# A graph block: rank and packed-edge tiles of 128 lanes in place of 125, and edge sends that use all of them

## The chip, the cores and the metric

The kernel runs on one core of a Trainium2 chip. The metric is the device time of one execution in microseconds (us); lower is better. The core has five engines that run side by side: TensorE (PE in the profile, its weight loads PEld), VectorE (DVE), ScalarE (ACT), GpSimd (POOL) and SyncE (SP), and 16 DMA engines that move data for all of them.

## The reference, cut to what matters

A block over a graph of 6,250 nodes with 256 features and 100,000 edges (`src`, `dst`), sorted by `dst`. Three of its steps read neighbours:

```
agg = segment_sum(relu(x[src]), dst)            # twice, in two graph convolutions, edges by dst
e   = exp(leaky_relu(el[src] + er[dst]))        # once, graph attention, grouped by src
out[src] += e / rowsum[src] * x[dst]
```

Between them stand dense steps on all nodes: two small MLPs, a mixing step, a linear layer with a layer norm, linear attention, and at the end a mixture of experts. The convolutions want the edges in the order of `dst`, the graph attention wants them in the order of `src`.

## The kernel before, in words

The 6,250 nodes are 49 tiles of 128 rows, the last one with 106 (`TAIL`). The kernel is a chain of stages (class `Stage`); at the end of each stage all engines meet at a barrier (line 48), so a stage lasts until its slowest engine is through.

An edge is one 32-bit word, `src << 13 | dst`. All 100,000 words lie in the tile `packed`, 125 partitions ("lanes", `LANES`) by 800 columns (`COLS`), written by VectorE at the end of `stage_load` (lines 281 to 283). The place that each edge takes in the list ordered by `src` is its rank. VectorE and TensorE work it out during the first convolution and leave it in `rank_i`, 125 by 800 too (line 1143).

The edges are then written out in that order, one column at a time: `send_columns` (line 676) issues on GpSimd an indirect DMA (a scatter) per column, with 125 indices from `rank_i[:, j]` and 125 words of 4 bytes from `packed[:, j]`, to `edges_by_src` in DRAM. The 800 columns are dealt out by hand to nine dense stages that otherwise leave GpSimd free; the calls in `stages_before_attention` (lines 2571 to 2583) give first column and count:

```python
stage_mlp(nc, m, "mlp1", m.w11s, m.b11s, m.w12s, m.b12r, False, (0, 136))
...
stage_mix(nc, m, (136, 8))
stage_mlp(nc, m, "mlp2", m.w21s, m.b21s, m.w22s, m.b22r, True, (144, 144))
stage_stats(nc, m, "stats1", 1e-5, columns=(288, 16))
stage_ffn(nc, m, (304, 80))
stage_stats(nc, m, "stats2", 1e-5, with_rms=True, columns=(384, 16))
stage_attn_kv(nc, m, (400, 152))
stage_attn_q(nc, m, (552, 160))
stage_attn_add(nc, m, (712, 88))
```

In each of these stages GpSimd does nothing but its sends and then waits until they have landed. It sends in batches of 8 columns; before batch g it waits that batch g-2 has landed. `stage_slots` behind them reads `edges_by_src` back, and the graph attention (`stage_gat`) starts from it. The second convolution (`conv2`) stands between `mlp1` and `stage_mix` and gathers with GpSimd, with no sends.

Other indirect DMAs are issued in the same way, with 128 indices: the gathers of the convolutions (line 1079) and of the attention (line 1852), the scatter of node rows to experts (line 2333) and the gather of their results (line 2508). The last two go tile by tile and take `[0:rows]`, which is 106 for the last tile.

If the edges come unsorted, `stage_begin` takes another path with the class `Scatter`; with these inputs it is not taken.

Of the kernel before, what the change touches and what calls it, by code (L numbers as in the profile page):

```python
# [5 lines left out]
P = 128  # L6
N, D = 6250, 256
E = 100000
EDGE_ROOM = (E + 2 * P - 1) // P * P
# [3 lines left out]
LANES = 125  # L13
COLS = E // LANES
CH = 10
CT = CH * TILES
BITS = 13
NOWHERE = (1 << BITS) - 1
# [120 lines left out]
def cols(t, start, width):  # L139
    return t[:, bass.ds(start, width)]  # L140
# [14 lines left out]
def stage_load(nc, m):  # L155
    with Stage(nc, "load") as st:
# [56 lines left out]
        @block.gpsimd  # L213
        def _(pool):
            nc.gpsimd.memset(m.next_i[:, :], NOWHERE).then_inc(next_set, 1)
            nc.gpsimd.memset(m.X[:, (TILES - 1) * D:TILES * D], 0.0).then_inc(x_clear, 1)
            for t, v in ((m.ident, 0.0), (m.tri, 1.0), (m.ones, 1.0), (m.zeros, 0.0), (m.mask64, 1.0), (m.mask32, 1.0)):
                nc.gpsimd.memset(t[:, :], v)
            nc.gpsimd.memset(pad_dst[:, :], NOWHERE)
            nc.gpsimd.memset(pad_src[:, :], NOWHERE << BITS)  # L220
            pool.drain().then_inc(pads, 1)
            nc.gpsimd.affine_select(out=m.ident[:, :], in_=m.ident[:, :], compare_op=ALU.not_equal, fill=1.0, base=0,
                                    pattern=[[-1, P]], channel_multiplier=1)

            nc.gpsimd.affine_select(out=m.tri[:, :], in_=m.tri[:, :], compare_op=ALU.is_ge, fill=0.0, base=-1,
                                    pattern=[[1, P]], channel_multiplier=-1)
            for t, w in ((m.mask64, 64), (m.mask32, 32)):
                v = t[:, :].rearrange("p (g j) -> p g j", j=w)
                nc.gpsimd.affine_select(out=v, in_=v, compare_op=ALU.is_ge, fill=0.0, base=0,
                                        pattern=[[-w, P // w], [0, w]], channel_multiplier=1)  # L230
                pool.drain()
                nc.gpsimd.affine_select(out=v, in_=v, compare_op=ALU.is_ge, fill=0.0, base=w - 1,
                                        pattern=[[w, P // w], [0, w]], channel_multiplier=-1)
            nc.gpsimd.iota(m.iota_row[:, :], [[1, P]], base=0, channel_multiplier=0, allow_small_or_imprecise_dtypes=True)
            nc.gpsimd.iota(m.slot_no[:, :], [[P, SC]], base=0, channel_multiplier=1, allow_small_or_imprecise_dtypes=True)
            pool.drain().then_inc(consts, 1)
# [41 lines left out]
        @block.vector  # L278
        def _(v):
            v.wait_ge(loaded, count[0])  # L280
            nc.vector.tensor_scalar(m.packed[:, :], src_i[:, :], BITS, None, ALU.logical_shift_left)
            v.drain()
            nc.vector.tensor_tensor(m.packed[:, :], m.packed[:, :], dst_i[:, :], ALU.bitwise_or)

# [362 lines left out]
class Scatter:  # L649
# [7 lines left out]
    def columns(self, pool, first, count):  # L657
        def batch(c, s):
            if reused(c):
                pool.wait_ge(self.sent[s], (c - s) * 64)  # L660
                held(pool, self.turns)
            self.nc.gpsimd.tensor_copy(self.idx[:, s, :], cols(self.m.rank_i, c * 8 + first, 8)).then_inc(self.copied, 1)
            self.nc.gpsimd.tensor_copy(self.pay[:, s, :], cols(self.m.packed, c * 8 + first, 8)).then_inc(self.copied, 1)
            pool.wait_ge(self.copied, c * 2 + 2)
            held(pool, self.turns)
            for k in range(8):
# [23 lines left out]
def stage_begin(nc, m):  # L690

    with Stage(nc, "begin") as st:
# [30 lines left out]

        @block.vector
        def _(v):
            nc.vector.tensor_scalar(key_i, m.packed[:, :], BITS + 7, None, ALU.logical_shift_right)
            v.drain()
            nc.vector.tensor_copy(m.key[:, :], key_i).then_inc(src_keys, 1)
            v.drain()
            nc.vector.tensor_scalar(key_i, m.packed[:, :], NOWHERE, 7, ALU.bitwise_and, ALU.logical_shift_right)  # L730
            v.drain()
            nc.vector.tensor_copy(key[:, :], key_i)
            v.drain()
# [23 lines left out]
            with v.If(v.value_load(m.unsorted[0:1, 0:1], min_val=0, max_val=1) != 0):  # L757
# [12 lines left out]
                    chunk(q * 2 + 1, 1)  # L770
                chunk(CHUNKS - 2, 0)
                chunk(CHUNKS - 1, 1)
                nc.vector.tensor_copy(m.rank_i[:, :], key[:, :]).then_inc(ranked, 1)
            nc.vector.tensor_scalar(bin_f2[:, :], bin_f[:, :], -float(P), None, ALU.mult)
            v.drain().then_inc(off_made, 1)

# [161 lines left out]
        def _(sp):  # L938
# [3 lines left out]
                             allow_slow_non_contiguous=True).then_inc(bin_stored, 16)  # L942
                sp.wait_ge(bin_stored, 16 * (which + 1))

            sp.dma_start(m.edges[0][0:E].rearrange("(p c) -> p c", p=LANES), m.packed[:, :]).then_inc(as_is, 16)
            sp.wait_ge(as_is, 16)
            bins_out(0)
            sp.dma_start(m.bin_row[:, :], m.bin_dram[0].rearrange("(a c) -> a c", a=1)).then_inc(bin_in, 16)
# [68 lines left out]
def stage_conv(nc, m, name, table, rank_sources, sum_keys):  # L1017
# [4 lines left out]
    with Stage(nc, name) as st:  # L1022
# [92 lines left out]
        def _(v):  # L1115
# [24 lines left out]
                kv.dve_norm(v, tv, TILES - 1)  # L1140
                kv.dve_end(v)
            if rank_sources:
                nc.vector.tensor_copy(m.rank_i[:, :], m.key[:, :])

        @block.tensor
        def _(pe):
# [1398 lines left out]
def stages_before_attention(nc, m, dense):  # L2545

    def sb(name, shape, dt=F32):
        return dense.enter_context(nc.sbuf_tensor(name, shape, dt))
# [1 line left out]
    m.next_i = sb("next_i", [LANES, 1], I32)  # L2550
    m.unsorted = sb("unsorted", [1, 1], I32)
    m.key = sb("key", [LANES, COLS])
    m.rank_i = sb("rank_i", [LANES, COLS], I32)
    m.base = sb("base", [P, CH, TILES])
    m.off_i, m.bin_f = sb("off_i", [P, SC], I32), sb("bin_f", [P, SC])
    m.kvbd = sb("kvbd", [P, 2, P + 4])
# [30 lines left out]
def stages(nc, m):  # L2587

    with ExitStack() as graph:
        def sb(name, shape, dt=F32):  # L2590
            return graph.enter_context(nc.sbuf_tensor(name, shape, dt))

        m.packed = sb("packed", [LANES, COLS], I32)
        m.GI = sb("GI", [P, SC * P], I32)
        m.LOC = sb("LOC", [P, SC * P])
        m.bin_row = sb("bin_row", [1, SC * P], I32)
# [25 lines left out]
def gps_program(nc, args, out):  # L2622
    with ExitStack() as ctx:
# [17 lines left out]
        m.xm = dram("xm", [NPAD, D])  # L2641
        m.expert_in = dram("expert_in", [EX_TILES * P, D])
        m.expert_out = dram("expert_out", [EX_TILES * P, D])
        m.edges = [nc.dram_tensor(f"edges_by_{e}", [EDGE_ROOM], I32).ap() for e in ("dst", "src")]
        m.bin_dram = [nc.dram_tensor(f"bins_by_{e}", [SC * P], I32).ap() for e in ("dst", "src")]

        m.X = sb("X", [P, TILES * D])
# [46 lines left out]
```

## Time and profile before

| what | value |
|---|---|
| time, median of 3 runs | 5827.18 us (5826.33 to 5827.49) |
| time of the profiled execution | 5832.27 us |
| its span, first to last instruction | 5830.6 us |
| granted TensorE clock, mean | 0.776 of full speed |
| GpSimd busy | 3751.5 us, 64% of the span |
| TensorE busy | 3310.6 us, 57% |
| VectorE busy | 2746.3 us, 47% |
| ScalarE busy | 2082.9 us, 36% |
| first send to last send issued | 1380.2 to 3692.4 us, `conv2` between 1585 and 2665 |

How to read it: a share of the span is a mean over all stages. The nine stages with sends each have a limit of their own, and it is read from which engine is still at work when the others already wait for the barrier.

### The profile page before, as it was taken

How to read it: one execution, taken by the hardware profiler on the slowest of the kernel's cores; microseconds unless marked ns; L12 is line 12 of the kernel's file. 1: busy time of each engine (PE TensorE's matmuls, PEld its weight loads, DVE VectorE, ACT ScalarE, POOL GpSimd, SP SyncE). 2: the span in 40 equal slices, each digit the busy share in tenths (PEclk: the TensorE clock that was granted, in tenths of full speed). 3: DMA queues.
4: the chain of work that ended last, by engine and by line, in shares of the span. 5: the costliest groups of instructions: out<-in, count | busy, mean ns of one | idle time of the engine just before them, and what ended most of it. 6: DMA issues, size and time to landing. Idle time of an engine off the chain costs nothing. (4 is left out here: it accounts for less than half of the span.)

```text
span 5830.6 us, 75495 instructions
## 1 busy us (share of the span) xinstructions
PE 3310.6 (57%) x13479; PEld 2372.5 (41%) x13480; DVE 2746.3 (47%) x6682; ACT 2082.9 (36%) x5020; POOL 3751.5 (64%) x3707
## 2 busy tenths in 40 slices
PE   4356656656466666667448360266666663149990
PEld 1134444444344444446437360144444443126660
DVE  6655555532245555544454265355555559202223
ACT  4433333333233333332113110255555545113331
POOL 4277777776777777776777777677777773520006
PEclk8577787778788888888789695588888875569995
DMA  2233333333133333342102120111111133341114
GB/s 76 92 98 103 103 103 102 104 104 55 38 111 111 110 109 110 110 106 39 30 1 48 23 33 1 17 27 27 27 27 27 27 26 124 105 147 54 56 55 134
DMA packets 280618, 407.59 MB, mean 70 GB/s; under 512 B 93991, under 2 KB 197765, under 8 KB 280262
## 3 DMA queue, kind: packets, MB, share of 16 engines
q0 software_dynamic: 142720, 275.10, 20.3%
q1 hardware_dynamic: 137798, 131.50, 7.3%
q14 instruction: 80, 0.66, 0.0%
q8 instruction: 20, 0.33, 0.0%
HBM read 323.82 MB, written 81.61 MB: 70 GB/s over the span
## 5 line engine op out<-in xcount | busy, mean ns | idle before, releaser
L1156 PE MATMUL conv_ps<-conv_msg,conv_S 128*128 128x256 f32 x3328 | 1157.7, 516 | 833.0 <-DMA conv_msg<-relu_xn_table,GI 423.7
L1156 PEld LDWEIGHTS conv_ps<-conv_msg,conv_S 128*128 128x128 f32 x3328 | 857.4, 268 | 1160.6 <-issue 988.7
L1128 DVE TENSOR_TENSOR ACC<-ACC,conv_ps 128x256 f32 x1664 | 700.8, 421 | 986.7 <-PE conv_ps L1156 859.3
L683 POOL DMA_INDIRECT edges_by_src<-packed,rank_i x800 | 954.9, 1194 | 309.2 <-issue 241.0
L1079 POOL DMA_INDIRECT conv_msg<-relu_xn_table,GI x832 | 799.1, 960 | 331.2 <-issue 262.3
L1852 POOL DMA_INDIRECT gat_msg<-attn_table,GI x832 | 826.7, 994 | 266.6 <-issue 253.3
L1079 POOL DMA_INDIRECT conv_msg<-conv_table,GI x832 | 789.4, 949 | 274.5 <-issue 262.9
L1905 PE MATMUL gat_ps<-gat_M,gat_S 128*128 128x260 f32 x1664 | 604.8, 511 | 367.4 <-DVE ACC L1959 218.5
L1099 ACT ACTIVATE conv_S<-iota_row,LOC 128x128 f32<-128x128 f32 x1664 | 507.9, 388 | 790.1 <-PE conv_ps L1156 706.0
L1905 PEld LDWEIGHTS gat_ps<-gat_M,gat_S 128*128 128x128 f32 x1664 | 377.8, 247 | 515.7 <-issue 460.1
L2508 POOL DMA_INDIRECT combine_y<-expert_out,combine_at x98 | 94.6, 965 | 579.6 <-ACTq L2496 559.2
L1959 DVE TENSOR_TENSOR ACC<-ACC,gat_ps 128x260 f32 x832 | 351.2, 422 | 58.5 <-PE gat_ps L1905 24.6
L1863 ACT ACTIVATE gat_SB<-iota_row,LOC 128x128 bf16<-128x128 f32 x832 | 254.2, 387 | 172.7 <-PEq L48 145.8
L1998 DVE TENSOR_TENSOR gat_M<-gat_msg,gat_M 128x512 f32<-128x512 f32 x416 | 285.3, 686 | 2.9 <-ACT gat_M L1889 2.9
L2471 DVE TENSOR_TENSOR experts_hb<-experts_ph,B1E 128x512 f32<-128x512 f32 x106 | 73.3, 692 | 436.9 <-PE experts_ph L2420 436.9
L1102 ACT ACTIVATE conv_S<-conv_S,ones 128x1024 f32<-128x1024 f32 x208 | 238.8, 1148 | 15.2
L2420 PE MATMUL experts_ph<-W1E,experts_xt 128*128 x424 | 213.2, 626 | 23.2 <-ACT experts_xt L2444 14.0
L1972 DVE TENSOR_REDUCE gat_zz<-gat_pel 128x32 f32<-128x96 f32 x104 | 26.8, 258 | 420.6 <-DMA gat_msg<-attn_table,GI 394.9
L1873 ACT COPY gat_ST<-gat_pst 128x1024 bf16<-128x1024 bf16 x104 | 105.2, 1012 | 326.3 <-PE gat_pst L1916 326.3
L2400 PE MATMUL experts_po<-W2E,experts_ht 128*128 x848 | 201.3, 380 | 1.0 <-ACT experts_ht L2437 1.0
L2400 PEld LDWEIGHTS experts_po<-W2E,experts_ht 128*128 128x128 f32 x848 | 161.8, 191 | 68.7 <-issue 52.0
L843 POOL TENSOR_TENSOR begin_oh<-key,iota_row 125x490 bf16<-125x490 f32 x80 | 94.5, 1191 | 113.1 <-PE begin_hist L862 68.0
(428 smaller groups left out, 5122.6 us busy)
## 6 DMA issues: line engine op xcount, KB each, us to landing
expert_in<-heads_zrow SPq DMA_DIRECT2D x53, 256.0 KB
experts_xe<-expert_in SPq DMA_DIRECT2D x106, 128.0 KB
expert_out<-experts_y SPq DMA_DIRECT2D x106, 128.0 KB, 1.7
conv_msg<-relu_xn_table,GI POOLq DMA_INDIRECT x832, 2.7
conv_msg<-conv_table,GI POOLq DMA_INDIRECT x832, 2.8
gat_msg<-attn_table,GI POOLq DMA_INDIRECT x832
edges_by_src<-packed,rank_i POOLq DMA_INDIRECT x800, 3.1
relu_xn_table<-begin_rx SPq DMA_DIRECT2D x49, 128.0 KB, 1.7
```

The source lines that it names most:

```text
L683: pool.indirect_dma_start(edges, bass.IndirectOffsetOnAxis(ap=m.rank_i[:, j:j + 1], axis=0), m.packed[:, j:j + 1], None).then_inc(sent[g % ...
L1079: pool.indirect_dma_start(msg[:, h * RING + k, :], None, table, bass.IndirectOffsetOnAxis(ap=m.GI[:, t:t + 1], axis=0)).then_inc(got[h] if ...
L1099: nc.scalar.activation(S[:, h, k, :], m.iota_row[:, :], ACT.Square, bias=cols(m.LOC, r * RING + k, 1), scale=-1.0)
L1102: nc.scalar.activation(half, half, ACT.Relu, bias=m.ones[:, 0:1], scale=-1.0).then_inc(s_made, 1)
L1128: nc.vector.tensor_tensor(acc, acc, ps[k % NB][:, 0:D], ALU.add).then_inc(added, 1)
L1156: nc.tensor.matmul(ps[k % NB][:, 0:D], S[:, h % 2, k, :], msg[:, h * RING + k, :], start=True, stop=True).then_inc(summed, 1)
L1852: pool.indirect_dma_start(msg[:, h * RING + k, :], None, m.attn_table, bass.IndirectOffsetOnAxis(ap=m.GI[:, t:t + 1], axis=0)).then_inc(go ...
L1863: nc.scalar.activation(SB[:, h, k, :], m.iota_row[:, :], ACT.Square, bias=cols(m.LOC, r * RING + k, 1), scale=-1.0)
L1905: nc.tensor.matmul(bank, S[:, h % 2, k, :], M[:, h * RING + k, :], start=True, stop=True).then_inc(summed, 1)
L1959: nc.vector.tensor_tensor(acc, acc, bank_of(h, k), ALU.add).then_inc(added, 1)
L1998: last = nc.vector.tensor_tensor(Mg[:, :, 64 * q:64 * q + 64], msg[:, g1 * RING:(g1 + 1) * RING, 0:64], Mg[:, :, D + q:D + q + 1].broadcas ...
L2400: mm = nc.tensor.matmul(po[s][:, 0:D], ht[s][:, c * P:c * P + P], cols(m.W2E, e * (4 * D) + c * D, D), start=(c == 0), stop=(c == 3))
```

## The change

`packed` and `rank_i` get all 128 partitions. The three new lanes are filled once in `stage_load` by GpSimd: `packed` is set to 0, and an iota writes into `rank_i` places that lie behind the list (`SIDE` + column, 800 for each new lane), so that `edges_by_src` grows from 100,224 to 102,656 words. VectorE waits for that before it packs the edges. Everything that works on the 125 lanes of edges now names them (`[0:LANES, ...]`), with the same shapes as before. `send_columns` itself is not edited: it takes `m.rank_i[:, j:j + 1]` and `m.packed[:, j:j + 1]`, which are now 128 lanes, so each of the 800 sends carries 128 indices and words in place of 125, three of them to places that nothing reads. The path for unsorted edges keeps 125.

```diff
 CH = 10
+SIDE = EDGE_ROOM
+SIDE_END = SIDE + ((P - LANES) * COLS + P - 1) // P * P
...
             nc.gpsimd.memset(pad_src[:, :], NOWHERE << BITS)
+            nc.gpsimd.memset(m.packed[:, :], 0)
+            nc.gpsimd.iota(m.rank_i[:, :], [[1, COLS]], base=SIDE - LANES * COLS, channel_multiplier=COLS)
             pool.drain().then_inc(pads, 1)
...
             v.wait_ge(loaded, count[0])
-            nc.vector.tensor_scalar(m.packed[:, :], src_i[:, :], BITS, None, ALU.logical_shift_left)
-            v.drain()
-            nc.vector.tensor_tensor(m.packed[:, :], m.packed[:, :], dst_i[:, :], ALU.bitwise_or)
+            v.wait_ge(pads, 1)
+            nc.vector.tensor_scalar(m.packed[0:LANES, :], src_i[:, :], BITS, None, ALU.logical_shift_left)
+            v.drain()
+            nc.vector.tensor_tensor(m.packed[0:LANES, :], m.packed[0:LANES, :], dst_i[:, :], ALU.bitwise_or)
...
-                nc.vector.tensor_copy(m.rank_i[:, :], m.key[:, :])
+                nc.vector.tensor_copy(m.rank_i[0:LANES, :], m.key[:, :])
...
-    m.rank_i = sb("rank_i", [LANES, COLS], I32)
+    m.rank_i = sb("rank_i", [P, COLS], I32)
...
-        m.packed = sb("packed", [LANES, COLS], I32)
+        m.packed = sb("packed", [P, COLS], I32)
...
-        m.edges = [nc.dram_tensor(f"edges_by_{e}", [EDGE_ROOM], I32).ap() for e in ("dst", "src")]
+        m.edges = [nc.dram_tensor(f"edges_by_{e}", [n], I32).ap() for e, n in (("dst", EDGE_ROOM), ("src", SIDE_END))]
```

## Rows read from the trace of the kernel before

**Rows 1.** The page: span, busy time of each engine, and the costliest group of sends.

```profile
span 5830.6 us, 75495 instructions
...
PE 3310.6 (57%) x13479; PEld 2372.5 (41%) x13480; DVE 2746.3 (47%) x6682; ACT 2082.9 (36%) x5020; POOL 3751.5 (64%) x3707
...
L683 POOL DMA_INDIRECT edges_by_src<-packed,rank_i x800 | 954.9, 1194 | 309.2 <-issue 241.0
```

**Rows 2.** Timeline: first work after a barrier; in brackets that engine's idle time before.

```profile
1585.25 0.27 DVE L1135 MEMSET conv_vn<- 128x258 f32 x1 [46.01 <-PEq L48]
...
2900.41 0.75 DVE L307 BATCH_NORM_STATS2 stats_parts<-X  x2 [52.12 <-PEq L48]
...
2928.12 0.73 DVE L1352 TENSOR_SCALAR ffn_xn<-X,mean,rstd 128x256 f32<-128x256 f32 x2 [9.00 <-PEq L48]
...
3053.34 0.75 DVE L307 BATCH_NORM_STATS2 stats_parts<-X  x2 [31.91 <-PEq L48]
...
3081.38 0.55 DVE L1433 MEMSET akv_vp<- 128x258 f32 x2 [7.38 <-PEq L48]
...
3316.38 0.43 DVE L1691 TENSOR_SCALAR aq_low<-aq_pq 128x256 f32<-128x256 f32 x1 [81.90 <-PE aq_pq L1613]
...
3556.44 1.79 DVE L1759 BATCH_NORM_STATS2 aadd_parts<-ACC  x5 [82.84 <-PEq L48]
...
3698.24 0.17 DVE L988 TENSOR_SCALAR slots_bin_f<-bin_f 128x7 f32<-128x7 f32 x1 [44.69 <-PEq L48]
```

**Rows 3.** Timeline: last send of three stages, and ScalarE around the end of `mix`.

```profile
1580.80 1.18 POOL L683 DMA_INDIRECT edges_by_src<-packed,rank_i  x1 [0.30 <-issue]
...
2676.33 1.18 POOL L683 DMA_INDIRECT edges_by_src<-packed,rank_i  x1 [0.30 <-issue]
...
2677.05 0.65 ACT L514 COPY mixM<-mix_pm 128x256 f32<-128x256 f32 x2 [3.87 <-PE mix_pm L503]
2680.54 0.71 ACT L1202 COPY mlp_hs<-ACC 128x256 f32<-128x256 f32 x2 [2.85 <-PEq L48]
...
3076.02 1.18 POOL L683 DMA_INDIRECT edges_by_src<-packed,rank_i  x1 [0.30 <-issue]
```

**Rows 4.** All sends of line 683: ns min/median/max, first and last start, time to landing.

```profile
L683 POOL DMA_INDIRECT edges_by_src<-packed,rank_i x800: 1172/1181/1552, 1380.2 to 3692.4; - x160
...
DMA to landing us min/median/max: 2.6/3.1/3.6
```

**Rows 5.** Windows of line 683: from:to, length, POOL busy (count), clock, DMA share, GB/s.

```profile
1379.40:1585.00 205.60, 160.65 (x136) 0.88 0.18 32
...
2900.00:2928.00 28.00, 18.86 (x16) 0.50 0.07 1
...
3556.00:3698.00 142.00, 110.18 (x88) 0.50 0.07 1
```

**Rows 6.** Other indirect DMAs, almost all of 128 lanes: ns min/median/max, starts.

```profile
L1079 POOL DMA_INDIRECT conv_msg<-conv_table,GI x832: 940/946/1177, 1585.9 to 2644.9; - x167
...
L2333 POOL DMA_INDIRECT expert_in<-dispatch_xm,dispatch_at x98: 967/971/1562, 5019.4 to 5143.8; - x98
...
L2508 POOL DMA_INDIRECT combine_y<-expert_out,combine_at x98: 942/946/1575, 5695.4 to 5817.9; - x98
```

**Rows 7.** Timeline of POOL: lines 2333 and 2508 where the tile of 106 rows comes.

```profile
5140.61 0.97 POOL L2333 DMA_INDIRECT expert_in<-dispatch_xm,dispatch_at  x1 [0.30 <-issue]
5141.89 1.56 POOL L2333 DMA_INDIRECT expert_in<-dispatch_xm,dispatch_at  x1 [0.31 <-issue]
...
5816.05 1.57 POOL L2508 DMA_INDIRECT combine_y<-expert_out,combine_at  x1 [0.30 <-issue]
```

**Rows 8.** Timeline of the load stage: two POOL operations, and VectorE's first packing operation.

```profile
1.53 0.54 POOL L218 MEMSET zeros<- 128x520 f32 x1
...
4.99 0.25 POOL L234 IOTA iota_row<- 128x128 f32 x1
...
28.29 0.58 DVE L281 TENSOR_SCALAR packed<-load_src_i 125x800 int32<-125x800 int32 x1 [28.15 <-DMA vbr<-in_L_mix_ln_v_b_dram]
```

More of the change, by code:

```diff
@@ L661, in batch @@
                 held(pool, self.turns)
-            self.nc.gpsimd.tensor_copy(self.idx[:, s, :], cols(self.m.rank_i, c * 8 + first, 8)).then_inc(self.copied, 1)
-            self.nc.gpsimd.tensor_copy(self.pay[:, s, :], cols(self.m.packed, c * 8 + first, 8)).then_inc(self.copied, 1)
+            self.nc.gpsimd.tensor_copy(self.idx[:, s, :], cols(self.m.rank_i[0:LANES, :], c * 8 + first, 8)).then_inc(self.copied, 1)
+            self.nc.gpsimd.tensor_copy(self.pay[:, s, :], cols(self.m.packed[0:LANES, :], c * 8 + first, 8)).then_inc(self.copied, 1)
             pool.wait_ge(self.copied, c * 2 + 2)
@@ L725, in _ @@
         def _(v):
-            nc.vector.tensor_scalar(key_i, m.packed[:, :], BITS + 7, None, ALU.logical_shift_right)
+            nc.vector.tensor_scalar(key_i, m.packed[0:LANES, :], BITS + 7, None, ALU.logical_shift_right)
             v.drain()
@@ L729, in _ @@
             v.drain()
-            nc.vector.tensor_scalar(key_i, m.packed[:, :], NOWHERE, 7, ALU.bitwise_and, ALU.logical_shift_right)
+            nc.vector.tensor_scalar(key_i, m.packed[0:LANES, :], NOWHERE, 7, ALU.bitwise_and, ALU.logical_shift_right)
             v.drain()
@@ L772, in _ @@
                 chunk(CHUNKS - 1, 1)
-                nc.vector.tensor_copy(m.rank_i[:, :], key[:, :]).then_inc(ranked, 1)
+                nc.vector.tensor_copy(m.rank_i[0:LANES, :], key[:, :]).then_inc(ranked, 1)
             nc.vector.tensor_scalar(bin_f2[:, :], bin_f[:, :], -float(P), None, ALU.mult)
@@ L943, in bins_out @@
                 sp.wait_ge(bin_stored, 16 * (which + 1))
-            sp.dma_start(m.edges[0][0:E].rearrange("(p c) -> p c", p=LANES), m.packed[:, :]).then_inc(as_is, 16)
+            sp.dma_start(m.edges[0][0:E].rearrange("(p c) -> p c", p=LANES), m.packed[0:LANES, :]).then_inc(as_is, 16)
             sp.wait_ge(as_is, 16)
```

## The prediction

> **What bounds the kernel now.** I read the page first. GpSimd is the busiest engine, and its costliest group is the 800 sends of line 683: 954.9 us busy, mean 1194 ns, with 309.2 us idle just before them [rows 1]. A mean over the span doesn't say whether that matters, so the next view is the timeline at the ends of the nine stages that send. The first instruction after each barrier carries the idle time of its engine. VectorE had been idle for 46.0 us when `conv2` began (behind `mlp1`), 52.1 behind `mlp2`, 9.0 behind `stats1`, 31.9 behind `ffn`, 7.4 behind `stats2`, 81.9 behind attention K/V (its first work there waits some us more for a load and a product), 82.8 behind attention Q and 44.7 behind `stage_attn_add` [rows 2]. Meanwhile GpSimd was sending: `mlp1`'s last send starts at 1580.80 us, `stats2`'s at 3076.02 [rows 3]. In `mix` ScalarE ends at 2677.70 (2677.05 + 0.65), while the last send, started at 2676.33, lands 3.1 us later at 2679.4 [rows 3, 4]. So all nine stages end with a send landing, followed by a barrier of 1.1 us (`mix`) to some 3.3 us (attention Q). A us taken off a send comes off the end, as long as the compute doesn't take over.
>
> The send costs 1181 ns in the median, plus about 0.30 us of issue [rows 3, 4]. The DMA engines don't set this pace: in `stats1`, where nothing else moves data, they are busy 7% of the time [rows 5].
>
> **What the change costs in the load stage.** A memset of 128 x 800 and an iota of 128 x 800. The nearest rows are a memset of 520 columns at 0.54 us and an iota of 128 columns at 0.25 us [rows 8]; scaled by columns they give 0.83 and at most 1.6 us. Some 2.4 us more before GpSimd signals at about 2.8 us, while VectorE is held by the weight loads until 28.29 us [rows 8]: the new wait is met long before. The constants reach ScalarE 2.4 us later, again under the loads. Cost 0; if that cover were gone, 2.4 us. The `[0:LANES]` views leave shapes as they were: 0.
>
> **What a send of 128 lanes costs.** This is the sum. The trace of before has no send of 128 words, so I bound it with other indirect DMAs. Gathers of 128 lanes take 946 ns, the scatter of 128 node rows to experts 971 ns [rows 6]. That alone could be the payload and not the lane count. What decides it for me is the last tile: the same two lines, with 106 lanes instead of 128, take 1.56 and 1.57 us [rows 7]. Fewer lanes cost more, so something in the number itself counts. 128 splits into 16 equal shares of 8; 125 at best into 5 of 25; 106 at best into 2 of 53 (divisors up to 16, the number of DMA engines). If a DMA costs a fixed part plus a part for each lane in a share, the scatter gives (1562 - 971) / (53 - 8) = 13.1 ns per lane of a share, the gather (1575 - 946) / 45 = 14.0. From 8 to 25 lanes a share, the scatter line would give 971 + 17 x 13.1 = 1194 ns and the gather line 946 + 17 x 14.0 = 1184; the sends in fact take 1181 [rows 4]. Two lines drawn without the sends land within 1.1% of them, at 4 bytes a lane against 1024. So I take the send off by 17 x 13.1 = 223 ns (the scatter is the nearest kind), to 958 ns. Bounds: to the 971 ns of the scatter, 210 ns saved; by the gather's slope, 238 ns.
>
> The Trainium skill, in "DMA: Bandwidth & Descriptors", section "Why a DMA increments its semaphore by 16 and not by 1", states the count that I inferred: the largest number up to 16 that divides the slowest dimension; by that rule the sum stays as it is. The same section speaks against this change too: it says that for some direct copies the software path takes 16 engines with the partitions rounded up per engine, which would give 125 lanes shares of 8 already, and a sum of nothing, 5827. The 106-lane rows go with the first rule.
>
> **By stage**, count x 0.223 us: `mlp1` 136, 30.3 us; `mix` 8, 1.8; `mlp2` 144, 32.1; `stats1` 16, 3.6; `ffn` 80, 17.8; `stats2` 16, 3.6; K/V 152, 33.9; Q 160, 35.7; `attn_add` 88, 19.6. Sum 178.4 us. Against the cover: VectorE's idle less a barrier of at most 3.3 us leaves 42.7, 48.8, 5.7, 28.6, 4.1, over 70, 79.5 and 41.4 us for all but `mix`; each is more than its saving. In `mix` the compute is 2679.4 - 2677.7 = 1.7 us ahead of the landing, so 1.7 of its 1.8 come through. Sum 178.3.
>
> The landing may shrink too: it is 3.1 us for a send. If the share of 8 shortened it by 0.4 us beyond the issue time, nine stage ends would give 3.6 us. I can't tell that from a row of the same kind; I take half, 1.8 us. GpSimd's excess over the median, 954.9 - 800 x 1.181 = 10.1 us, is mostly in `attn_add` (110.18 / 88 = 1.252 us a send against 18.86 / 16 = 1.179 in `stats1`) [rows 1, 4, 5], beside VectorE's work there; I leave it as it is. No other stage changes: `conv2`, the attention and the experts gather with their own 128 lanes.
>
> Total: 178.3 + 1.8 = 180 us. The profiled execution itself took 5832.27 us, so 5652; the median of the runs is 5.1 us below that execution, which puts the forecast at 5827.2 - 180 = 5647 us. By the bounds: 800 x 0.210 = 168 us gives 5659; 800 x 0.238 + 3.6 = 194 gives 5633.
>
> **The rivals.**
> - *Compute takes over in the tight stages*, because barriers or the last stores take longer than I read. `mix`, `stats1` and `stats2` hold 9 us of savings together, `ffn` 17.8. Losing half of these 27 us gives 5660. For it: 4.1 us of cover against 3.6 in `stats2`. Against it: the idle rows. Chance 0.06.
> - *The sends stay at 1.18 us*, since the 4-byte words or the 16-way split with rounding up set their price, and the coincidence of two lines is one. Then three more lanes at no visible cost: 5827. The 106-lane rows speak against it, the missing row of a 128-word send leaves it open. Chance 0.03.
> - *The other sign: a price per word.* If the send is paid by lanes, 1181 / 125 = 9.4 ns each, three more are 28 ns, x 800 = 23 us: 5850. It decides from the point where the after-send is over 1181 ns. For it: sends are dearer than 128-lane gathers though they have fewer lanes and bytes. Against it: 1.57 us at 106 lanes. The same sign would come if writes of single words on 16 engines queued up, so that batch g waited for batch g-2; at 7% DMA busy, rising to about 7% x 1.484 / 1.261 x 128 / 125 = 8.4%, there is a long way to go. Chance 0.03.
>
> **How the numbers follow.** The forecast has 0.88: 5647 us, with its own range 5633 to 5660. The first rival ends at 5660 and in part lies inside it. The range 5631 to 5664 takes both ends of the send's price, 2 us below for a landing that shrinks more, and 4 us above for cover lost; it leaves out somewhat under 2 in 10. A change of less than 0.2% (12 us) can't be told from none here. Faster 0.94, same 0.03, slower 0.03.
>
> **What the profile after would show.** The group of line 683 at a median near 0.96 us, in steps of 1.26 us, and 190 us less GpSimd busy at most. VectorE idle before the barriers shorter by exactly the savings: some 16 us behind `mlp1`, 5 to 6 behind `stats1`, 25 behind `attn_add`; `mix` within 1 us of ending on ScalarE. `conv2` to begin about 30 us earlier and to last as long. The load stage to end at the same time. The prediction would be wrong if a send stayed above 1.1 us, if batches waited for each other, or if `conv2` or the attention stage changed in length.

## The result, and the profile after

The changed kernel takes 5677.0 us in the median of 3 runs (5676.58 to 5678.78), against 5827.18 before: ratio 0.9741, 95% interval 0.9728 to 0.9754. It is faster by 150.2 us. The forecast was 180 us, and 5677 lies outside the range. The direction was right, the size was not. The profiled execution took 5676.58 us, 155.7 less than the profiled one of before.

The page after shows what the change was to do (span, busy time by engine, the group of sends; the lines have moved by five, L683 is now L688):

```profile
span 5674.6 us, 75498 instructions
...
PE 3289.9 (58%) x13479; PEld 2361.4 (42%) x13480; DVE 2740.0 (48%) x6682; ACT 2083.7 (37%) x5020; POOL 3574.8 (63%) x3709
...
L688 POOL DMA_INDIRECT edges_by_src<-packed,rank_i x800 | 781.0, 976 | 325.5 <-issue 252.4
```

The sends of line 688, ns min/median/max, and first and last start:

```profile
L688 POOL DMA_INDIRECT edges_by_src<-packed,rank_i x800: 963/969/1230, 1379.4 to 3535.2; - x160
```

The send went from 1181 to 969 ns [rows 4], and the group's busy time from 954.9 to 781.0 us [rows 1]: 173.9 us. But the idle time just before the sends rose from 309.2 to 325.5 us, though a send's issue still takes 0.30 us. That is the first sign that something else grew.

The idle time of VectorE at the first work after a barrier, as in [rows 2], behind `mlp1`, `mlp2`, `stats1`, `ffn`, `stats2`, Q and `attn_add`:

```profile
1558.65 0.27 DVE L1140 MEMSET conv_vn<- 128x258 f32 x1 [19.36 <-PEq L50]
...
2845.77 0.43 DVE L312 BATCH_NORM_STATS2 stats_parts<-X  x1 [26.93 <-PEq L50]
...
2869.75 0.73 DVE L1357 TENSOR_SCALAR ffn_xn<-X,mean,rstd 128x256 f32<-128x256 f32 x2 [5.35 <-PEq L50]
...
2981.27 0.43 DVE L312 BATCH_NORM_STATS2 stats_parts<-X  x1 [18.22 <-PEq L50]
...
3005.62 0.55 DVE L1438 MEMSET akv_vp<- 128x258 f32 x2 [3.80 <-PEq L50]
...
3422.13 2.12 DVE L1764 BATCH_NORM_STATS2 aadd_parts<-ACC  x6 [54.34 <-PEq L50]
...
3545.84 0.17 DVE L993 TENSOR_SCALAR slots_bin_f<-bin_f 128x7 f32<-128x7 f32 x1 [25.98 <-PEq L50]
```

Behind `stats1` the idle time is 5.35 us; [rows 2] less the forecast saving gives 5.4. Behind `stats2` 3.80 against 3.8. The small stages went as forecast. Behind `mlp1` there are 19.4 us where 15.7 were due, behind `mlp2` 26.9 where 20.0 were, behind `ffn` 18.2 where 14.1 were, behind Q 54.3 where 47.1 were, and behind `attn_add` 26.0 where 25.1 were. The long stages end later than their sends explain. What fills the time is in two views. The first is the timeline of GpSimd in `mlp1`. Its 114th send starts at 1525.30 us, 2.10 us behind the end of the 113th, where 0.30 us is the usual gap; such a gap is called a pause here:

```profile
1522.23 0.97 POOL L688 DMA_INDIRECT edges_by_src<-packed,rank_i  x1 [0.30 <-issue]
1525.30 0.97 POOL L688 DMA_INDIRECT edges_by_src<-packed,rank_i  x1 [2.10 <-issue]
1526.57 0.96 POOL L688 DMA_INDIRECT edges_by_src<-packed,rank_i  x1 [0.30 <-issue]
```

The second is the end of `ffn`: GpSimd's queue alone, at the barrier's DRAIN, and the busy time of all engines in that stretch (from:to, length, PE, PEld, DVE, ACT, POOL busy with counts, clock, DMA share, GB/s):

```profile
L48 POOLq DRAIN  x1: 6582/6582/6582, 2973.6 to 2973.6; - x1
...
2972.00:2981.30 9.30, 0.00 (x0) 0.00 (x0) 0.03 (x1) 0.00 (x0) 0.10 (x1) 0.50 0.00 0
```

The last send of `ffn` starts at 2971.13, GpSimd's wait for its landing (line 691) is over at 2973.44, and then the DRAIN that begins the barrier takes 6.58 us, in which no engine works and no DMA moves. Before, the same DRAIN took 1.355 us:

```profile
L46 POOLq DRAIN  x1: 1355/1355/1355, 3050.9 to 3050.9; - x1
```

All nine stages, read in the same two views. A stage's length runs from the last semaphore of one barrier on GpSimd to that of the next:

| stage, sends | DRAIN before, us | DRAIN after | pause after | stage shorter by | forecast |
|---|---|---|---|---|---|
| `mlp1` 136 | 0.70 | 2.01 | 2.10 | 25.9 | 30.3 |
| `mix` 8 | 0.70 | 0.70 | - | 1.6 | 1.8 |
| `mlp2` 144 | 1.35 | 2.66 | 2.05 | 27.0 | 32.1 |
| `stats1` 16 | 1.35 | 1.35 | - | 3.7 | 3.6 |
| `ffn` 80 | 1.35 | 6.58 | - | 13.7 | 17.8 |
| `stats2` 16 | 1.35 | 1.35 | - | 3.7 | 3.6 |
| K/V 152 | 2.01 | 3.31 | 2.02 | 29.0 | 33.9 |
| Q 160 | 2.66 | 3.96 | 2.58 | 29.6 | 35.7 |
| `attn_add` 88 | 2.01 | 7.24 | - | 18.1 | 19.6 |
| sum | 13.5 | 29.2 | 8.75 | 152.3 | 178.4 |

The whole span is 156.0 us shorter. The other 3.7 us lie in stages that don't send, 2.3 of them in the graph attention, whose length differs by 2.6 us between executions that all send 125 lanes (1109.8 to 1112.4).

Each pause stands behind the 113th send of its stage. "Cleared" is a word for what is inferred here: GpSimd keeps something for each DMA that it issued, and gets rid of it at certain points. With it the DRAINs after fit one line: 0.05 us plus 0.0817 us for each DMA that isn't cleared yet. `stats1` has 16 such: 1.35. `ffn` 80: 6.58. `attn_add` 88: 7.24. Where the pause was, 112 are cleared: `mlp1` keeps 136 - 112 = 24, 2.01 us; Q 48, 3.96. With 125 lanes the DRAINs fit multiples of 64 that are cleared on the way, with no pause to be seen: `ffn` 80 - 64 = 16, 1.35; Q 160 - 128 = 32, 2.66. So the line is the same in both kernels, and the change moved the places where GpSimd clears.

Both were in the trace of before, at other lines. The gathers of 128 lanes in the convolution pause there too, behind the 113th, and `dispatch`, with 98 DMAs, ends with a DRAIN of 8.06 us = 0.05 + 98 x 0.0817. Timeline of GpSimd, and GpSimd's DRAIN at line 46, both before:

```profile
441.09 1.00 POOL L1079 DMA_INDIRECT conv_msg<-relu_xn_table,GI  x1 [0.30 <-issue]
443.76 0.94 POOL L1079 DMA_INDIRECT conv_msg<-relu_xn_table,GI  x1 [1.67 <-issue]
```

```profile
L46 POOLq DRAIN  x1: 8064/8064/8064, 5152.9 to 5152.9; - x1
```

Not every DRAIN can be read so. The one behind the first convolution is recorded with 14.1 us, but its record begins while GpSimd still has gathers to do: the last one ends at 1365.59, and only 7.4 us come after it. The attention gathers with 128 lanes as well and has no pause at all, and 14.2 us of its DRAIN of 29.7 stand behind its last gather, more than the line gives for any backlog seen elsewhere. These stages don't fit the account, and why is open.

```profile
L46 POOLq DRAIN  x1: 14122/14122/14122, 1358.8 to 1358.8; - x1
...
1364.64 0.95 POOL L1079 DMA_INDIRECT conv_msg<-relu_xn_table,GI  x1 [0.30 <-issue]
```

### The profile page after: what moved, and what is told of

It reads as the page before. It is cut to its first block and busy times, and to the rows that moved or that the text cites. A ratio compares the mean times of both kernels' runs of the same rounds, so it can differ in the third digit from the quotient of the medians.

```text
span 5674.6 us, 75498 instructions
## 1 busy us (share of the span) xinstructions
PE 3289.9 (58%) x13479; PEld 2361.4 (42%) x13480; DVE 2740.0 (48%) x6682; ACT 2083.7 (37%) x5020; POOL 3574.8 (63%) x3709
## 3 DMA queue, kind: packets, MB, share of 16 engines
q0 software_dynamic: 142720, 274.23, 19.6%
## 5 line engine op out<-in xcount | busy, mean ns | idle before, releaser
L688 POOL DMA_INDIRECT edges_by_src<-packed,rank_i x800 | 781.0, 976 | 325.5 <-issue 252.4
L2456 ACT ACTIVATE experts_hg<-experts_hb 128x512 f32<-128x512 f32 x106 | 66.8, 630 | 268.7 <-DVE experts_hb L2476 268.7
```

What stands on the lines that cost most here:

```text
L688: pool.indirect_dma_start(edges, bass.IndirectOffsetOnAxis(ap=m.rank_i[:, j:j + 1], axis=0), m.packed[:, j:j + 1], None).then_inc(sent[g % ...
```

## The experiments

The experiments ran on five chips. On three of them the kernel before takes 5828 to 5829 us; on two it takes 6977 to 6983. The second kind is told of at the end of this section. Where a run has no ratio, it is a single execution. Ratios are always to the kernel before on the same chip.

**The changed kernel again, `e0_after`.** No edit.

> The changed kernel once more, beside the experiments. Its profile on record has sends at 969 ns, one pause of 2.0 to 2.6 us behind the 113th send in each of the four stages with more than 113 sends, and at the ends of stages a DRAIN of GpSimd that takes 0.70 us after 8 sends, 1.35 after 16, 6.58 after 80 (ffn), 7.24 after 88 (attn_add), and 2.01, 2.66, 3.31, 3.96 in the stages that paused. If these belong to the kernel and not to that one execution, they come again within 0.1 us, and the time is 5677 us within 5.

5675.0 us, ratio 0.9741 [0.9725, 0.9757]. The same nine DRAINs to 0.01 us, the pauses 2.0 to 2.7 us, behind the 113th again.

**125 lanes of the 128, `e1_125_of_128`.** Only the send's operands:

```
-  IndirectOffsetOnAxis(ap=m.rank_i[:, j:j + 1], ...), m.packed[:, j:j + 1]
+  IndirectOffsetOnAxis(ap=m.rank_i[0:LANES, j:j + 1], ...), m.packed[0:LANES, j:j + 1]
```

> Undoes one part: the tiles keep 128 lanes, their initialisation and the larger list, but each send takes lanes 0 to 124. If the lane count of the send is everything (my theory), the sends are back at 1181 ns, the pauses are gone, the drains are back at 0.7 to 2.7 us, and the time is 5827 us within 0.1%. If the longer list in DRAM, the rows of the initialisation or the three rows of the tiles do something, the time lands apart from 5827 by more than 6 us, or the drains stay at 6.6 and 7.2 us.

5827.93 us, ratio 0.9999 [0.9989, 1.0008]. The sends of that kernel:

```profile
L688 POOL DMA_INDIRECT edges_by_src<-packed,rank_i x800: 1172/1180/1437, 1380.8 to 3692.2; - x160
```

The DRAINs are those of before. So memset, iota, wait and longer list cost nothing that can be measured, and the whole effect, the gain and what is missing of it, comes with the lane count of the sends. `e13_125_elsewhere` and `e16_125_again` are the same kernel on two further chips:

> The changed kernel with its sends on lanes 0 to 124 only; ranks and edges keep 128 lanes. On a chip where the kernel before takes 5827: ratio 1.000 as before. On a chip where it takes 6980: if the loss of the changed kernel there lies in its sends alone, 1.000 too (6980 us); rival, if it comes from where the code or the tiles lie now, near 1.06.

0.9996 [0.9987, 1.0006].

> The changed kernel with its sends on lanes 0 to 124 only. On a chip where the kernel before takes 5829: ratio 1.000. On a chip where it takes 6980: 1.000 too, if the loss of the changed kernel there lies in its sends alone; rival, if it comes from where code or tiles lie now, near 1.06.

0.9997 [0.9988, 1.0007].

**Nine lane counts, `e2_lane_sweep`.** Each stage sends with a lane count of its own; where lanes are missing the list is filled from the unsorted one, so that the rest runs.

```
+    lanes = {0: 120, 136: 126, 144: 112, 288: 127, 304: 124, 384: 121, 400: 96, 552: 64, 712: 100}[first]
-  ap=m.rank_i[:, j:j + 1]   m.packed[:, j:j + 1]
+  ap=m.rank_i[0:lanes, j:j + 1]   m.packed[0:lanes, j:j + 1]
```

> Leaves edges out: each stage sends only the first n lanes of its columns, n by stage: mlp1 120, mix 126, mlp2 112, stats1 127, ffn 124, stats2 121, K/V 96, Q 64, attn_add 100 (the list is filled beforehand with the edges as they are). Theory of shares, 853 ns + 13.1 ns for each lane in a share, with as many shares as the largest divisor up to 16: 120 (15 of 8) 958 ns, 126 (14 of 9) 971, 112 (16 of 7) 945, 127 (1 of 127) 2517, 124 (4 of 31) 1259, 121 (11 of 11) 997, 96 (16 of 6) 932, 64 (16 of 4) 905, 100 (10 of 10) 984. Rival, a price by lanes alone: all between the values of 64 and 128 lanes in the order of the lane count, 127 next to 128 at about 0.98 us. For the drains: if a drain pays for each DMA, about 82 ns each, whatever its lanes, then 80 sends of 124 lanes leave 6.6 us and 88 of 100 lanes 7.2; if it pays for entries in a ring that fills by the share, 64 lanes (5 entries with the one for the semaphore, against 9) leave a drain about half as long for each send and the pause comes at about 200 sends, so not at all in Q.

5705.81 us. Sends of line 689 in windows of `mlp1` (120 lanes), `stats1` (127), `ffn` (124) and Q (64); the window cuts one or two sends off some stages or adds one of the next, so the medians count and not the extremes:

```profile
L689 POOL DMA_INDIRECT edges_by_src<-packed,rank_i x136: 978/983/1112, 1378.0 to 1554.8; - x136
...
L689 POOL DMA_INDIRECT edges_by_src<-packed,rank_i x16: 939/2536/2545, 2836.0 to 2884.9; - x16
...
L689 POOL DMA_INDIRECT edges_by_src<-packed,rank_i x78: 1302/1309/2543, 2891.0 to 3021.3; - x78
...
L689 POOL DMA_INDIRECT edges_by_src<-packed,rank_i x159: 892/897/1135, 3239.3 to 3439.1; - x159
```

| lanes | shares | median ns | forecast | DRAIN us | not cleared |
|---|---|---|---|---|---|
| 120 | 15 x 8 | 983 | 958 | 2.01 | 24 of 136, pause 2.29 at 113 |
| 126 | 14 x 9 | 980 | 971 | 0.70 | 8 of 8 |
| 112 | 16 x 7 | 936 | 945 | 2.01 | 24 of 144 |
| 127 | 1 x 127 | 2538 | 2517 | 0.12 | 1 of 16, pauses 3.6 and 3.5 at 7 and 15 |
| 124 | 4 x 31 | 1309 | 1259 | 0.70 | 8 of 80 |
| 121 | 11 x 11 | 1007 | 997 | 1.35 | 16 of 16 |
| 96 | 16 x 6 | 911 | 932 | 2.66 | 32 of 152 |
| 64 | 16 x 4 | 897 | 905 | 3.31 | 40 of 160 |
| 100 | 10 x 10 | 981 | 984 | 7.24 | 88 of 88 |

127 lanes, one fewer than 128, take 2.6 times as long. The nine sizes are within 4% of the share law, and its order holds but for 120 lanes, which take 983 ns where 126 take 980 and 100 take 981; a price per word can't give it. The shares can also be seen directly. The trace records each packet of the DMA engines with its size, and a send's packets hold one share of 4-byte words: 100 B (25 words) with 125 lanes, 32 B (8 words) with 128 and 120, and in the sweep 36, 28, 124, 44, 24, 16 and 40 B for 126, 112, 124, 121, 96, 64 and 100 lanes. With 127 lanes they are 256 and 252 B, together 127 words. (Each send shows 16 packets of its size, also where the rule gives 5 shares; nothing here accounts for that.) The median packet takes 116 ns with 125 lanes and 15 ns with 128.

The Trainium skill states the rule of the divisor in "DMA: Bandwidth & Descriptors", section "Why a DMA increments its semaphore by 16 and not by 1"; by that rule, the runs agree. The exception that the Trainium skill states in the same section for some direct copies (partitions rounded up on each engine) would have left 127 lanes near 969 ns; it doesn't show in these indirect DMAs.

The DRAIN's price per DMA doesn't depend on lanes (88 DMAs: 7.24 with 100 lanes and with 128). Even the 127 lanes fit: behind the pauses at the 7th and the 15th send one of the 16 is left, for which the line gives 0.13 us, and the DRAIN takes 0.12:

```profile
L48 POOLq DRAIN  x1: 122/122/122, 2896.7 to 2896.7; - x1
```

Where GpSimd clears does depend on lanes: shares of 7, 6 and 4 cleared 120 without a pause, shares of 31 cleared 72, shares of 8 cleared 112 with one. What sets these points is open. `e14_sweep_elsewhere` and `e17_sweep_again` are the same kernel on two further chips:

> Lanes of a send by stage: 120, 126, 112, 127, 124, 121, 96, 64, 100 (the lists of edges are not complete for most, filled from the unsorted ones). Send medians 983, 980, 936, 2538, 1309, 1007, 911, 897, 981 ns on any chip. On a chip of the slow kind the lengths of the stages tell shape from rate: if it is 16 shares that delay the other engines, mlp2 (112 lanes, 16 shares of 7) and K/V (96) and Q (64) last 340 to 360 us as in the changed kernel there, and mlp1 (120 lanes, 15 shares of 8) and ffn (124, 4 shares) less, near 231 and 125; if it is the rate of the sends, mlp1 (983 ns a send) lasts about 328 as well, and ffn (1309 ns a send) alone comes down.

5704.54 us, all medians within 3 ns of the first sweep's.

> Lanes of a send by stage: 120, 126, 112, 127, 124, 121, 96, 64, 100 (the lists of edges are filled from the unsorted ones where lanes are missing). On a chip of the slow kind: if it is 16 shares that delay the other engines, mlp2 (112 lanes in 16 shares), K/V (96) and Q (64) last 340 to 360 us as in the changed kernel there, and mlp1 (120 lanes, 15 shares) and ffn (124 lanes, 4 shares) less, near 231 and 125; if it is the rate of the sends, mlp1 (983 ns a send) lasts about 328 as well and ffn (1309 ns a send) alone comes down. On a chip of the other kind it repeats what is known: 5705 us.

5703.88 us. Both came to chips of the first kind, so they say nothing on the second.

**No waits between batches, `e3_no_batch_waits`.** The prediction had named this way to be wrong.

```
-        if g >= 2:
-            pool.wait_ge(sent[g % 2], g // 2 * 128)
```

> Takes away the wait of batch g for batch g-2 in the sends; the waits at the end stay. Rival: the sends run into this wait, which is what I had named as a way to be wrong; then the four pauses behind the 113th send go and some 7 us with them, 5670. Theory: the pause is GpSimd's own and comes at the same send, and the drains stay as they are; time as the changed kernel within 0.1%.

5677.29 us, ratio 0.9744 [0.9727, 0.976]. The pauses stay at the 113th (2.0 to 3.4 us), the DRAINs too. This rival falls: the pause is not the wait for batch g-2.

**Other dealing, `e12_dealt_120_third`.** If the DRAIN's time is paid for DMAs not cleared, part of it can be had back by ending stages just behind a clearing. Only the counts of columns change:

```
- 136, 8, 144, 16,  80, 16, 152, 160,  88
+ 136, 8, 136, 16, 120, 16, 120, 128, 120
```

> Sends dealt 136, 8, 136, 16, 120, 16, 120, 128, 120 over the nine stages. On a chip where the kernel before takes 5827: by the theory that a stage's end pays 82 ns for each DMA not cleared, the nine DRAINs sum to 10 us in place of 29 and two pauses come on top, so 14.7 us under the changed kernel, 5662 us, ratio 0.9716; rival (another engine's end takes over, or the DRAIN's time only moves): 0.974 or more. On a chip of the slow kind: 1.064, no statement.

5660.15 us, ratio 0.9712 [0.9699, 0.9725]. The end of `ffn` and of `attn_add`:

```profile
L48 POOLq DRAIN  x1: 702/702/702, 3013.4 to 3013.4; - x1
...
L48 POOLq DRAIN  x1: 702/702/702, 3527.8 to 3527.8; - x1
```

120 sends end with a DRAIN of 0.70 us, where 80 ended with 6.58. The nine DRAINs sum to 10.9 us in place of 29.2, six pauses stand in place of four, and the nine stages together last 1071.5 us in place of 1086.6: 15.1 less, forecast 14.7. The expectation of 5662 is met within 2 us, and this is the fastest kernel of the study. This kernel and the changed one ran on different chips, so they are compared by their ratios (0.9712 and 0.9741); the intervals touch at 0.9725, so what shows the gain is the stages and DRAINs, with the medians in agreement.

The same dealing and one more were tried on a chip of the second kind, where sends don't set the ends of the stages:

> The changed kernel with its 800 columns dealt out anew: 136, 8, 136, 16, 120, 16, 120, 128, 120 for mlp1, mix, mlp2, stats1, ffn, stats2, K/V, Q, attn_add (it was 136, 8, 144, 16, 80, 16, 152, 160, 88). Theory: GpSimd keeps something for each DMA it issued; it clears 112 of them in the pause behind the 113th send (1.8 us beyond the issue), and what is left is worked off in the DRAIN at the end of the stage at 82 ns each. Left over: 24, 8, 24, 16, 8, 16, 8, 16, 8, 128 in all against 352, so drains shorter by 18.3 us, two pauses more for 3.6 us: 14.7 us faster than the changed kernel, near 5662. The drains of ffn and attn_add fall from 6.58 and 7.24 us to 0.70 each. Rival, a drain that waits for the backlog of all sends of the stage: ffn and attn_add with 120 sends would have drains of 9.8 us, and the time would not fall.

7423.7 us, ratio 1.0637 [1.062, 1.0654]; DRAINs 2.01, 0.70, 2.01, 1.35, 0.70, 1.35, 0.70, 1.35, 0.70.

```
- 136, 8, 144, 16,  80, 16, 152, 160,  88
+ 136, 8, 136, 16, 112, 16, 128, 136, 112
```

> The partner of the kernel with 120: only 16 columns stand elsewhere (136, 8, 136, 16, 112, 16, 128, 136, 112), so that ffn and attn_add stop one send short of the pause. Theory: 112 sends each are left there, drains of 9.2 us; left over in all 24 + 8 + 24 + 16 + 112 + 16 + 16 + 24 + 112 = 352, as many as in the changed kernel, and four pauses: the time of the changed kernel, 5677, and 14.7 us more than the partner. Rival, drains in proportion to all sends of the stage: ffn and attn_add some 0.7 us shorter than in the partner, K/V and Q as much longer, and the two kernels take the same time.

7429.81 us, ratio 1.0647 [1.0629, 1.0665]; `ffn` and `attn_add` end with DRAINs of 9.20 us, as 112 uncleared DMAs give (0.05 + 9.15). Eight sends more and the DRAIN falls from 9.20 to 0.70: the theory holds for the DRAINs; the times of these two say nothing on their worth.

**Does waiting clear? `e6_idle_and_mid_drain`.** 96 sends in `mlp1`, then GpSimd waits for the compute before the barrier; in `ffn` a DRAIN behind the 40th send; 200 sends in Q.

```
-  mlp1 (0, 136) ...  Q (552, 160)
+  mlp1 (0, 96)  ...  Q (512, 200)
+        if count == 80 and g == 5:
+            pool.drain()
+            if not last:
+                pool.wait_ge(out_made, TILES)
```

> Three looks in one kernel, columns dealt 96, 8, 144, 16, 80, 16, 152, 200, 88. In mlp1 GpSimd has only 96 sends and then waits for the last tile of the compute, some 35 us without work, before its DRAIN. Theory: the rest is not worked off while it waits, DRAIN 96 x 0.082 + 0.05 = 7.9 us. Rival: GpSimd's processors lag behind their queue and catch up in the 35 us, DRAIN under 0.5 us. In ffn a DRAIN stands behind the 40th of 80 sends. Theory: 3.3 us there (more if it waits for the last landing too), 3.3 us at the end instead of 6.58. In Q, 200 sends: the second pause comes behind the 201st, so 88 are left, DRAIN 7.2 us; if it came at 2 x 112 or never, the same; if the DRAIN pays for all 200, 16.4 us.

7461.12 us, on a chip of the second kind, where the compute of `mlp1` ends late. GpSimd waited 151 us behind its 96th send, and the DRAIN of that stage still took 7.89 us (0.05 + 96 x 0.0817 = 7.89). In `ffn` the 40 DMAs cost 4.05 us of gap in the middle and 3.32 us at the end:

```profile
L48 POOLq DRAIN  x1: 7887/7887/7887, 1934.0 to 1934.0; - x1
...
3839.23 0.96 POOL L690 DMA_INDIRECT edges_by_src<-packed,rank_i  x1 [0.30 <-issue]
3844.24 0.97 POOL L690 DMA_INDIRECT edges_by_src<-packed,rank_i  x1 [4.05 <-issue]
```

So clearing isn't done while GpSimd waits on a semaphore, and the DRAIN doesn't wait for transfers, which land within 3.6 us by [rows 4]. What missed is Q: its 200 sends had one pause, as expected, but a DRAIN of 9.33 us where 7.2 were due. The 2.1 us more are about those of a pause, which may have fallen into the DRAIN; that isn't shown.

**Sends of 128 lanes, paced, `e11_paced` and `e15_paced_again`.**

```
+            nc.gpsimd.memset(m.pace[0:64, j:j + 1], 0)
+            nc.gpsimd.memset(m.pace[64:P, j:j + 1], 0)
```

> The changed kernel with two small MEMSETs on GpSimd behind each of the 800 sends (about 0.1 us each by the MEMSETs of one column at the start), so that a send comes every 1.4 to 1.5 us, as in the kernel before, and still has 128 lanes. Nothing is left out. On a chip where the kernel before takes 5827: the gain is eaten, about 5827 plus the 23 us of longer DRAINs and pauses less what a pause hides, 5830 to 5860, ratio 1.000 to 1.005. On a chip where the kernel before takes 6980 and the changed one 7436: if it is the rate of the sends that delays the other engines there, the stages beside the sends come down to about those of the kernel before (mlp1 231 us, mlp2 251) and the whole to 7000 to 7050; rival, if it is that a send of 128 lanes lies in 16 shares instead of 5, the stages stay at 330 to 345 us and the whole at 7400 or more.

> The changed kernel with two small MEMSETs behind each send (a send every 1.39 us in place of 1.27). On a chip where the kernel before takes 5829: 5771 us, ratio 0.990, as measured on such a chip. On a chip where it takes 6980 and the changed one 7436: if the rate of the sends delays the other engines there, mlp1 and mlp2 fall from 328 and 345 us about half way to the 231 and 251 of the kernel before, and the whole to some 7200; if their 16 shares do, they stay and the whole is 7400 or more.

5771.33 us, ratio 0.9902 [0.9887, 0.9917], and on another chip 5771.23 us, 0.9901 [0.9884, 0.9917]. The first expectation missed by 60 us, because the MEMSETs lie mostly in the 0.30 us of issue. Timeline of GpSimd:

```profile
1399.65 0.97 POOL L688 DMA_INDIRECT edges_by_src<-packed,rank_i  x1
1400.66 0.10 POOL L690 MEMSET pace<- 64x1 uint8 x1
1400.79 0.10 POOL L691 MEMSET pace<- 64x1 uint8 x1
1401.04 0.97 POOL L688 DMA_INDIRECT edges_by_src<-packed,rank_i  x1
```

A send comes every 1.39 us in place of 1.27. 800 x 0.115 = 92 us, and 5677 + 92 = 5769. So the interval of the sends goes into the time one for one, which is the frame of the forecast. What these two runs were made for, the chips of the second kind, they didn't meet.

**Chips of the second kind.** The changed kernel on one of them:

> The changed kernel beside the two other ways to deal out the columns, on the same chip: 5675 to 5677 us, ratio to the kernel before 0.974.

7437.5 us, ratio 1.0655 [1.0638, 1.0672]. On the other, first the dealt kernel of `e12_dealt_120_third`, then the changed kernel and the kernel before:

> Sends dealt in multiples of 8 that end near a clearing: 136, 8, 136, 16, 120, 16, 120, 128, 120 columns. Theory (the end of a stage pays 82 ns for each DMA not cleared): the nine DRAINs sum to about 10 us where the changed kernel's sum to 29; two stages more have the pause behind the 113th send (+4.6 us), so 14.7 us less than the changed kernel on a chip like the first: 5662 us, ratio 0.9716 against 0.9741. Rival (the DRAIN's time only moves, because the stage's end waits for landings anyway or because the other dealing makes another engine the bound): the same as the changed kernel, 0.974, or slower.

7431.57 us, ratio 1.0643 [1.062, 1.0667].

> The changed kernel itself, on the same chip as the two others of this call, for the comparison with the dealt one. On a chip like the first: ratio 0.974, 5677 us. On a chip like that of the second call: ratio 1.065 as there, and then the profile of the kernel before from this call shows which stages hold the difference.

7435.85 us, ratio 1.0654 [1.0632, 1.0677].

> The kernel before, unchanged, so that a profile of it stands beside the others on whatever chip this call gets. Ratio 1.000 by every theory. On a chip like the first its nine stages show sends of about 1180 ns, no pause, and DRAINs of 0.70 to 2.66 us. On a chip like that of the second call (6982 us) the sends and DRAINs are the same by the theory that GpSimd is not what is slower there; if instead the sends are longer there, that theory falls.

6986.73 us, ratio 1.0003 [0.9986, 1.0019]. On these chips the change makes the kernel 6.5% slower. The sends, DRAINs and pauses are the same as elsewhere, so the theory that GpSimd isn't what is slower there stands. The dealing of `e12_dealt_120_third` gave 4 us on this chip (7431.57 against 7435.85) and 14 us on the other (7423.7 against 7437.5); since other engines end most stages there, these differences are not read as its worth. The windows of `mlp1`, `ffn` and the experts, which have no indirect DMA (from:to, length, PE, PEld, DVE, ACT, POOL, clock, DMA share, GB/s), of the kernel before on such a chip, and of the changed one on the same chip:

```profile
1653.40:1884.00 230.60, 141.27 (x686) 113.36 (x686) 45.85 (x147) 64.06 (x196) 160.37 (x136) 0.83 0.15 29
...
3641.70:3766.70 125.00, 67.47 (x294) 43.87 (x294) 64.06 (x147) 18.26 (x49) 96.38 (x80) 0.87 0.08 1
6320.40:6840.30 519.90, 484.37 (x1908) 309.14 (x1908) 118.20 (x212) 169.61 (x319) 0.00 (x0) 0.98 0.17 53
```

```profile
1650.50:1978.00 327.50, 122.62 (x686) 99.00 (x686) 45.24 (x147) 64.20 (x196) 132.20 (x136) 0.73 0.07 20
...
3821.60:4005.00 183.40, 78.72 (x294) 49.44 (x294) 60.57 (x147) 18.23 (x49) 77.81 (x80) 0.69 0.01 0
6761.40:7280.80 519.40, 483.45 (x1908) 308.49 (x1908) 118.30 (x212) 169.49 (x319) 0.00 (x0) 0.99 0.17 54
```

The experts last as long as on the other chips (519.7 us). `mlp1` lasts 327.5 us with sends of 128 lanes and 230.6 with sends of 125; VectorE and ScalarE are busy equally long in both. Cut at the last send, `mlp1` shows when the time is lost (the kernel before up to its last send, then the changed one up to its last send and from there on):

```profile
1653.80:1856.20 202.40, 122.34 (x579) 98.57 (x580) 37.57 (x120) 54.62 (x167) 160.37 (x136) 0.81 0.16 27
```

```profile
1650.80:1826.80 176.00, 28.85 (x110) 23.20 (x110) 4.79 (x15) 10.59 (x31) 132.16 (x136) 0.56 0.03 4
1826.80:1978.30 151.50, 93.77 (x576) 75.80 (x576) 40.44 (x132) 53.62 (x165) 0.04 (x1) 0.93 0.11 38
```

Beside 136 sends of 125 lanes TensorE gets through 579 of its 686 matmuls; beside 136 sends of 128 lanes it gets through 110, and the other 576 come when the sends are over. An example of where the time goes is a late wake-up. Timeline of `mlp1` there: TensorE's products for ScalarE and VectorE are given by 1703.9, VectorE starts at 1709.6 and ScalarE at 1731.2:

```profile
1701.94 1.91 PE L1252 MATMUL mlp_po<-w12s,mlp_h 128*128 128x256 f32 x4
1709.62 0.42 DVE L1282 TENSOR_TENSOR mlp_b<-mlp_po,b12r 128x256 f32<-128x256 f32 x1 [34.85 <-DMA conv_msg<-relu_xn_table,GI]
...
1731.22 0.62 ACT L1224 ACTIVATE mlp_h<-mlp_ph,b11s 128x128 f32<-128x128 f32 x2 [31.79 <-DMA conv_msg<-relu_xn_table,GI]
```

The releaser in brackets can't be meant: those gathers ended with `conv1`, 50 us before. It is what the view names when no event near the end of the wait fits.

More sends make a stage longer there by their own time, though another engine ends it: `ffn` 183.4 us with 80 sends and 232.2 with 120 (1.22 us each), Q 363.9 with 160, 322.3 with 128 (1.30 each). It is as if sends of 128 lanes and the compute took turns. Both kernels' convolutions, which gather with 128 lanes beside the compute, are longer there in the same way: 1358 us for `conv1`, 1083 on the other chips. Whether it is the 16 shares or the higher rate of sends is open. The rate alone looks unlikely, since a send every 1.27 us in place of 1.48 brought the matmuls done beside them from 2.9 a us down to 0.6, but no run tests it. The paced kernel and the sweep were to tell, and both came to chips of the first kind. What differs in these chips is open as well.

## Why the prediction was wrong

**What bounds the kernel: right.** All nine stages still end with GpSimd; the paced kernels show the interval passing into the time one for one, 92 us for 800 x 0.115.

**"Cost 0" in the load stage: right.** 0.9999 with 125 of 128 lanes. Memset and iota took 0.76 and 0.79 us, under the loads.

**The law of shares: right, its size a little off.** The send came to 969 ns, not 958: 169.6 us in the medians instead of 178.3. The 971 ns row of the scatter [rows 6], which the prediction kept as its lower bound of saving, was the better one. GpSimd's excess over the median fell from 10.1 to 5.8 us (781.0 - 800 x 0.969), which the prediction had left as it is: 4.3 us given back. The last rival put the share of the DMA engines at "rising to about" 8.4%. That has the wrong sign: in `stats1` it fell from 7% to 2%, with packets of 15 ns in place of 116.

**"Each is more than its saving", the cover: right.** No engine took over; the small stages came out within 0.2 us, `mix` narrowly: ScalarE ends there 0.2 us before GpSimd's DRAIN does.

**The landing: about right.** From the last send's start to the DRAIN the nine stages take 23.6 us in place of 26.7; 1.9 of this is the shorter send itself, 1.1 remain where 1.8 were put.

**The step that failed** is the one that turned sends into stage ends: "So all nine stages end with a send landing, followed by a barrier of 1.1 us (`mix`) to some 3.3 us (attention Q). A us taken off a send comes off the end". The barrier was taken as fixed. It isn't: the 1.1 to 3.3 us were a DRAIN of 0.70 to 2.66 and 0.4 to 0.7 us of signals, and with 128 lanes the DRAIN is 0.70 to 7.24. That cost 15.7 us. And the count times 0.223 took all sends as alike; four stages have a pause behind the 113th, 8.75 us less four issues of 0.30, 7.5 us. The third and smaller part is the send itself, 969 ns where 958 were put, less what the excess gave back: 178.3 - 173.9 = 4.4 us. `e1_125_of_128` shows that DRAINs and pauses come with the lane count, `e6_idle_and_mid_drain` that the DRAIN counts DMAs and not landings, the dealt kernel that 18.3 us of the DRAINs can be had back for two pauses more. The sum on the rows: 173.9 - 15.7 - 7.5 + 1.1 = 151.8 us, against 152.3 by the stages and 150.2 by the medians. With the DRAINs and pauses in it, the forecast would have been 180 - 15.7 - 7.5 = 157 us, 5670.

The rival that came nearest was that the tight stages lose their savings; by its time, 5660, it was closer, but its mechanism is not what happened. The prediction's own sign of an error, batches that wait for each other, is refuted by `e3_no_batch_waits`. That 5647 would have been missed on any chip of the second kind is another matter: the prediction had one trace, from a chip of the first. The barrier's range from 1.1 to 3.3 us should have raised the question of what makes it vary: the DRAINs of line 46 hold the answer, in the trace of before.

## What to carry to other kernels

Choose the lane count of an indirect DMA by its largest divisor up to 16: here 128 or 112 lanes were cheap and 127 dear. On chips of the first kind a full tile with three dummy lanes beat 125 true ones by 2.6% of the kernel (5677 and 5675 us; on one further chip the dealt form by 2.9%), and on two of the second kind it lost 6.5%. Before costing a shorter instruction, read what stands between the last one's landing and the next stage's first work, and whether that varies between stages: a DRAIN on GpSimd paid 0.082 us for each indirect DMA not yet cleared. Where work is dealt over stages, end them just behind a clearing (120, not 112 or 80 DMAs of 128 lanes), and measure on more than one chip.

## What the runs showed of the hardware

- GpSimd's DRAIN takes 0.05 us + 0.0817 us per indirect DMA not cleared (1 to 112 of them, 0.12 to 9.20 us), with 64 to 128 lanes alike and though all have landed; it isn't worked off in 151 us of waiting on a semaphore. The DRAINs of the convolutions and of the attention don't fit, nor does that behind 200 sends (9.33 us).
- With shares of 8 lanes (128 and 120 lanes) GpSimd pauses 1.7 to 3.4 us behind the 113th DMA, and in the convolution's gathers every 88 after that; the attention's gathers of 128 lanes don't pause. With shares of 7 or fewer 120 are cleared without a pause, with shares of 25 multiples of 64, with shares of 31 72 of 80.
- A send of 127 lanes takes 2538 ns, one of 128 takes 969. Its packets hold one share each: 32 B with 128 lanes, 100 B with 125, 256 and 252 B with 127.
- On two of five chips the compute beside indirect DMAs takes much longer than on the other three, while the sends themselves take as long (970 ns): `conv1` 1358 us against 1083, `mlp1` with sends of 128 lanes 327.5 against 179.8, with sends of 125 lanes 230.6 against 205.8; the experts, without indirect DMAs, 520 on both.
